# Attention and expert block: order of the prologue, of the second step's sums, and of the x rows and zeros on SyncE's queue

## What is computed

```
q, k, v = x @ wq.T, x @ wk.T, x @ wv.T           # 16 heads of 128
q, k    = rope(rmsnorm(q) * qn), rope(rmsnorm(k) * kn)   # over the head's 128
s       = 50 * tanh(q @ k.T / sqrt(128) / 50);  causal mask
x       = layernorm(x + softmax(s) @ v @ wo.T)
logits  = x @ gate.T     # 32 experts in 8 groups: the 3 best groups, the 6 best experts
x       = layernorm(x + sum of 6 weighted experts (48 places each) + shared expert)
```

## Time and profile before

| | |
|---|---|
| timed runs | 1084.98, 1086.15, 1086.78 us; median 1086.15 |
| profiled execution | 1092.47 us, of which 1090.7 are the span of the trace |
| mean granted TensorE clock | 0.973 |
| TensorE (matmul) busy | 1019.1 us, 93% |
| DVE busy | 850.7 us, 78% |
| ScalarE busy | 698.9 us, 64% |
| GpSimd busy | 647.2 us, 59% |
| HBM read, written | 63.00 MB, 15.75 MB |

### The profile page before, as it was taken

The page is one execution under the profiler, slowest core; times in us unless marked ns, Lnnn a source line. Parts: engine busy times, 40 slices in busy tenths (PEclk is TensorE's granted clock), DMA queues, the critical chain, the costliest instruction groups (busy, mean ns, idle before and its releaser), DMA issues.

```text
span 1090.7 us, 17557 instructions
## 1 busy us (share of the span) xinstructions
PE 1019.1 (93%) x6072; PEld 809.2 (74%) x6072; DVE 850.7 (78%) x1391; ACT 698.9 (64%) x1162; POOL 647.2 (59%) x660
## 2 busy tenths in 40 slices
PE   7799999999999999999999999999999968899966
PEld 5588878887888788888878887888788747345532
DVE  6579898989898889888988898889988865833423
ACT  4667777777777777777777777777777752323212
POOL 2536666666666666666666666666666662365332
PEclk9999999999999999999999999999999987999987
DMA  5610011101110101010101000100000007739937
GB/s 193 238 30 20 31 39 30 62 30 39 31 61 30 41 30 61 31 40 30 62 30 40 31 20 30 40 30 20 21 20 21 21 1 227 209 86 265 237 55 235
DMA packets 52168, 75.42 MB, mean 69 GB/s; under 512 B 8208, under 2 KB 43248, under 8 KB 51952
## 3 DMA queue, kind: packets, MB, share of 16 engines
q1 hardware_dynamic: 48144, 69.30, 20.1%
q0 software_dynamic: 3072, 4.46, 2.2%
q10 hardware_dynamic: 864, 0.54, 0.2%
HBM read 63.00 MB, written 15.75 MB: 72 GB/s over the span
## 4 chain that ended last, share of the span: by engine, by line
PE 67%; DVE 16%; issue 6%; DMA 6%; POOL 2%; ACT 2%; SPq 0%; ACTq 0%; DVEq 0%; POOLq 0%
PE ps L462 19%; PE ps L463 18%; PE ps L464 18%; DVE prob_lo L1230 6%; PE ps L499 5%; DMA acc_rows<-ye,acci 4%; PE ps L676 2%; DVE qraw L1299 2%; POOL pacc L1089 2%; PE ps L720 2%; PE ps L767 1%; DVE qraw L1317 1%; DVE kT_lo L1230 1%; PE ps L716 1%; DVE qhat_lo L1230 1%
## 5 line engine op out<-in xcount | busy, mean ns | idle before, releaser
L1230 DVE TENSOR_TENSOR prob_lo<-praw,prob_hi 128x1024 fp32r<-128x1024 f32 (+7 forms) x256 | 301.4, 1201 | 3.4 <-ACT prob_hi L837 3.4
L1072 POOL TENSOR_SCALAR_AFFINE_SELECT praw<-praw 128x128 f32<-128x128 f32 x256 | 119.5, 467 | 264.4 <-ACT praw L893 261.6
L1089 POOL TENSOR_TENSOR pacc<-pacc,praw 128x768 f32<-128x768 f32 (+2 forms) x192 | 234.6, 1222 | 27.7
L887 ACT ACTIVATE praw<-ps,rk 128x1024 f32<-128x1024 f32 (+7 forms) x256 | 186.2, 741 | 68.8 <-PE ps L464 64.6
L837 ACT ACTIVATE prob_hi<-praw 128x1024 fp32r<-128x1024 f32 (+7 forms) x256 | 168.7, 686 | 1.9 <-POOL praw L1072 1.9
L893 ACT ACTIVATE praw<-praw 128x1024 f32<-128x1024 f32 (+7 forms) x256 | 168.2, 684 | 0.0
L462 PE MATMUL ps<-qhat_hi,kT_hi 128*128 128x512 f32 (+3 forms) x384 | 135.2, 352 | 9.6 <-DVE qhat_lo L1230 9.6
L462 PE MATMUL ps<-prob_hi,vS_hi 128*128 128x512 f32 (+3 forms) x384 | 136.4, 355 | 8.0 <-DVE prob_lo L1230 8.0
L463 PE MATMUL ps<-prob_lo,vS_hi 128*128 128x512 f32 (+3 forms) x384 | 133.9, 349 | 0.0
L464 PE MATMUL ps<-prob_hi,vS_lo 128*128 128x512 f32 (+3 forms) x384 | 133.0, 346 | 0.0
L463 PE MATMUL ps<-qhat_lo,kT_hi 128*128 128x512 f32 (+3 forms) x384 | 132.9, 346 | 0.0
(11 more groups left out here) (167 smaller groups left out, 2240.2 us busy)
## 6 DMA issues: line engine op xcount, KB each, us to landing
qsq<-rq_rows SPq DMA_DIRECT2D x32, 512.0 KB, 4.0
wgu<-in_wgu SPq DMA_DIRECT2D x16, 704.0 KB
wd<-in_wd SPq DMA_DIRECT2D x16, 352.0 KB
acc_rows<-acc_rows SPq DMA_DIRECT2D x8, 544.0 KB, 6.1
acc_rows<-pacc SPq DMA_DIRECT2D x8, 512.0 KB, 9.8
accA<-acc_rows SPq DMA_DIRECT2D x8, 512.0 KB, 5.8
wraw<-in_wqkv SPq DMA_DIRECT2D x15, 256.0 KB, 4.5
wvraw<-in_wqkv SPq DMA_DIRECT2D x16, 128.0 KB, 2.7
```

The lines of the kernel that those rows point to most:

```text
L887: nc.scalar.activation(praw[:, raw_at(b, j)], buf[:, P * j:T], ACT.Tanh, scale=rk[:, b, j:j + 1]).then_inc(tanh_done, 1)
L1072: nc.gpsimd.affine_select(out=diag, in_=diag, compare_op=ALU.is_ge, fill=0.0, base=0, pattern=[[1, P]], channel_multiplier=-1).then_inc(ma ...
L1089: nc.gpsimd.tensor_tensor(pacc[:, P * j:T], before, raw, ALU.add).then_inc(pacc_done, 1)
L1230: v.tensor_tensor(dst, x_, hi.bitcast(F32), ALU.subtract).then_inc(done, 1)
```

## The change

DVE's prologue runs the fold of q's sums right behind q1, and V's weights' split behind that; `turn_rms(0)` follows, then the head scales, then the second head's weights. In the opening, `ss` comes ahead of `vb` in the list, on TensorE ahead of the first scores, and on DVE (with the output weights' split and `turn_rms(1)`) ahead of vb's low part. SyncE loads x's rows behind the broadcast of the second row. Of the zeros the front keeps one write of 256 rows (256 KB) and the one of 144 KB. The other 16 parts of the first table and 17 of the second are copies of those 256 rows, six behind the last broadcast of each of the pairs 1 to 5 and three in pair 6; the first scatter waits for all 33.

```diff
--- before.py
+++ after.py
@@ -42,7 +42,10 @@
 XD = D + E
 ACCR = N + P
 ROUNDS = C // 8
-ZEROS = 16 * ((2 * ACCR // P * D + T - 1) // T + 1)
+ZEROS = 16 * 2
+PARTS = 17
+PART = 2 * ACCR // PARTS
+CLEARS = 2 * PARTS - 1
 NEG = -3.0e38
 POS = 3.0e38
 SR = 2
@@ -74,7 +77,7 @@
 BEHIND = {"sums", "op0", "op1", "op2", "op3"}
 AHEAD = {"q0", "q1", "k0", "k1", "ss"}
 PROLOGUE = "q0 q1 sq k0 k1 vd sk".split()
-OPENING = "k0 k1 va q0 q1 vb ss".split()
+OPENING = "k0 k1 va q0 q1 ss vb".split()
 EARLY = len(PROLOGUE) + len(OPENING)
 EARLY_BANKS = [6, 7, 4, 5]
 SMALL = 4
@@ -288,7 +291,7 @@
         xhi_done, xlo_done = sem("xhi_done"), sem("xlo_done")
         whi_done, wlo_done = sem("whi_done"), sem("wlo_done")
         wq_in, wqhi_done, wqlo_done = sem("wq_in"), sem("wqhi_done"), sem("wqlo_done")
-        sq_folded, side_zeros = sem("sq_folded"), sem("side_zeros")
+        sq_folded, table_zeros = sem("sq_folded"), sem("table_zeros")
         wohi_done, wolo_done = sem("wohi_done"), sem("wolo_done")
         pj_done, pj_free = sem("pj_done"), sem("pj_free")
         wvhi_done, wvlo_done, vhi_done = sem("wvhi_done"), sem("wvlo_done"), sem("vhi_done")
@@ -376,14 +379,15 @@
                 sp.dma_start(rqB[:, :], rq_d[b:b + 1, :].to_broadcast([P, T])).then_inc(rqB_in, 16)
 
             rq_broadcast(0, 0)
-            sp.dma_start(yacc[:, :, :], x_v).then_inc(x_in, 16)
             sp.wait_ge(zeros_set, 1)
             zero = pacc[:, :]
-            rows = acc_d.rearrange("(p r) d -> p (r d)", p=P)
-            for c0 in range(0, 2 * ACCR // P * D, T):
-                cn = min(T, 2 * ACCR // P * D - c0)
-                sp.dma_start(rows[:, c0:c0 + cn], zero[:, 0:cn]).then_inc(zeros_out, 16)
+            sp.dma_start(acc_d[0:PART, :].rearrange("(p r) d -> p (r d)", p=P), zero[:, 0:PART * D // P]).then_inc(zeros_out, 16)
             sp.dma_start(x1_d[N:ACCR, :], zero[:, 0:XD]).then_inc(zeros_out, 16)
+
+            def clear(n):
+
+                table, part = (acc_d, n + 1) if n < PARTS - 1 else (acc2_d, n - PARTS + 1)
+                sp.dma_start(table[PART * part:PART * part + PART, :], acc_d[0:PART, :]).then_inc(table_zeros, 16)
 
             next_wqkv = wqkv_d[2:H].rearrange("(n e) p m c d -> n e p m c d", e=2)
             next_wo = wo_d[2:H].rearrange("(n e) p d -> n e p d", e=2)
@@ -392,6 +396,8 @@
                 for e in range(2):
                     sp.dma_start(wvraw[:, e], next_wqkv[bass.ds(p, 1), e, :, 2].rearrange("o p c d -> p (o c) d")).then_inc(wv_in, 16)
                 rq_broadcast(p * STEPS + 1, 1)
+                if p == 0:
+                    sp.dma_start(yacc[:, :, :], x_v).then_inc(x_in, 16)
                 sp.wait_ge(wlo_done, p * 2 + 2)
                 for e in range(2):
                     sp.dma_start(wraw[:, e], next_wqkv[bass.ds(p, 1), e, :, 0:2].rearrange("o p m c d -> p (o m) c d")).then_inc(w_in[e], 16)
@@ -400,13 +406,12 @@
                 for e in range(2):
                     sp.dma_start(woraw[:, e], next_wo[bass.ds(p, 1), e].rearrange("o p n -> p (o n)")).then_inc(wo_in[e], 16)
                 rq_broadcast(p * STEPS + 3, 1)
-                if 1 <= p < 5:
-                    if p == 1:
-                        sp.wait_ge(zeros_out, ZEROS)
-                    for part in (2 * p - 2, 2 * p - 1):
-                        some = slice(ACCR // 4 * part, ACCR // 4 * part + ACCR // 4)
-                        sp.dma_start(acc2_d[some, :], acc_d[some, :]).then_inc(side_zeros, 16)
                 rq_broadcast(p * STEPS + 4, 0)
+                if p == 0:
+                    sp.wait_ge(zeros_out, ZEROS)
+                else:
+                    for n in range(6 * p - 6, min(6 * p, CLEARS)):
+                        clear(n)
             for q in range(1, STEPS):
                 rq_broadcast((NP_ - 1) * STEPS + q, q % 2)
 
@@ -575,12 +580,12 @@
                 pe.wait_ge(wlo_done, 2)
                 for what in OPENING[:-2]:
                     project(what, 0 if what[0] == "v" else 1, 0, *st.unit(what))
+                sums_of_squares(1, *st.unit("ss"))
                 pe.wait_ge(qlo_done, 1)
                 scores(0, 0, 0)
                 pe.wait_ge(xlo_done, 2 * KC + 1)
                 scores(0, 0, 1)
                 project("vb", 0, 0, *st.unit("vb"))
-                sums_of_squares(1, *st.unit("ss"))
                 for j in (2, 3, 4, 5):
                     scores(0, 0, j)
                 pe.wait_ge(pj_free, st.unit("q1")[0])
@@ -1180,12 +1185,12 @@
 
             def scatter(p):
                 pool.wait_ge(ey_evac, p + 1)
+                if p == 0:
+                    pool.wait_ge(table_zeros, 16 * CLEARS)
                 row = bass.IndirectOffsetOnAxis(ap=acci[:, p:p + 1], axis=0)
                 if p in SIDE:
                     if SIDE.index(p):
                         pool.wait_ge(side_added, 16 * SIDE.index(p))
-                    else:
-                        pool.wait_ge(side_zeros, 16 * 8)
                     nc.gpsimd.indirect_dma_start(acc2_d, row, ye[:, p % 4, :], None, compute_op=ALU.add).then_inc(side_added, 16)
                 else:
                     if MAIN.index(p):
@@ -1354,13 +1359,12 @@
             for h in range(2 * KC):
                 split_x(h)
             split_first_keys()
+            for what in ("q0", "q1", "sq"):
+                at_start(what)
+            split_values_weights(0, None)
+            turn_rms(0)
             head_gains()
-            at_start("q0")
-            split_values_weights(0, None)
-            at_start("q1")
-            at_start("sq")
             split_next_weights(0, 1, None)
-            turn_rms(0)
             for what in ("k0", "k1", "vd", "sk"):
                 at_start(what)
             split_x(2 * KC)
@@ -1409,10 +1413,11 @@
 
             def opening(st):
 
-                for what in ("va", "q0", "q1", "vb", "ss"):
+                for what in ("va", "q0", "q1", "ss"):
                     opens(st, what)
                 split_output_weights(st)
                 turn_rms(1)
+                opens(st, "vb")
                 for j in range(4):
                     tile(0, 0, j)
                 scale_raw(1, 1)
```

## The result

The kernel after took **1078.75 us** (median of 13 timed runs, 1075.91 to 1088.71) where the kernel before took 1087.34 (median of 13 beside them, 1081.23 to 1094.52). The ratio is 0.9932, 95% interval 0.9904 to 0.9959: 7.4 us faster, 4.5 to 10.4. The time lies 3.6 us above the predicted 1075.2, inside the range, and outside the 1074 to 1077 of the forecast itself. The sign was right and the size was too large: 11.0 us were forecast. Two of the later sets held one execution at a far lower granted clock (1254 us of before, 1445 us of e7), and these two are in no median or ratio here.

What follows compares the result with a forecast made beforehand. The prediction took the middle as bound by TensorE at a fixed pace, so front savings carry through; 11.6 - 0.6 = 11.0 us off the 1086.15 median gave 1075.2 us, range 1072.6 to 1079.2.

Steps and rivals of the forecast that it cites:

- the forecast itself: Whole kernel: 1074 to 1077 us around the point 1075.2, given a chance of 0.55.
- What bounds the kernel: Middle: TensorE at a fixed pace, 108.17 us a pair, so savings in the front move the rest one for one.
- Part 1: DVE's prologue: first row writes at 14.1, 2.1 us earlier, and scaled queries 2.2 us earlier.
- Part 2: Second step's sums ahead of first scores: first scores 1.67 us earlier, step 1's scores at 44.3, 10.0 us earlier.
- From there to the steady pace: Step 1's scores to V: V's projection at 47.1, clock gain 1.2, 11.6 us in all, less 0.6 for k1 waiting.
- Rival (e): Output weights' split in step 1 not disturbed: V at 45.7 and no 0.6, 1073.2 us; chance 0.12.
- Rival (a): Clock stays a problem: if it falls around the second scores, 2.4 us come back, 1077.6 us; chance 0.12.
- rival (b): Weights' split: each half waits for a whole GpSimd add of 2.11 us, V at 49.6, 1077.7 us; chance 0.04.
- Part 3: x rows behind the second row: loaded by 43.9 at the latest, when DVE comes; costs 0, up to 1 us.
- Part 4: Zeros moved to copies behind later pairs' last broadcasts: cost taken as 0, ends 0 and 3.3 us.
- the last one of the sum: Final step: 11.0 us off the profiled span also come off the 1086.15 median, as the front hardly differs.

Runs made afterwards that it cites:

- e7: Kernel after with each of the 33 zero copies followed by one more of 256 KB to an unused table; 1078.34 us, ratio 0.9919.
- e11: Kernel after with only DVE's old prologue put back (head scales and V's split ahead of q's sums); 1080.85 us, ratio 0.9936.
- e10: Kernel after with second step's sums back behind its third scores and x rows back behind the first broadcast; 1078.34 us, ratio 0.9917.
- e5: Kernel after with 18 and 12 small unread matmuls filling TensorE's pauses around attention's last sums; 1075.93 us, ratio 0.9910.
- e4: Kernel after with only the second step's sums put back between its third scores and V's unit; 1083.0 us, ratio 0.9975.
- e14: Kernel before, unchanged, fourth profile; no timed median given, last sums of attention at 898.50 us.
- e13: Kernel before, unchanged, third profile; no timed median given, last sums of attention at 894.37 us.
- e9: Kernel before, unchanged, second profile; no timed median given, last sums of attention at 895.74 us.
- e6: Kernel before with 18 and 12 small unread matmuls filling TensorE's pauses around attention's last sums; 1085.0 us, ratio 0.9981.
- e3: Kernel before with only the new orders of DVE and TensorE, x rows and all zeros staying in front; 1084.45 us, ratio 0.9978.
- e1: Kernel after, unchanged, timed and profiled a second time; 1078.55 us, ratio 0.9921.
- e15: Kernel after, unchanged, third profile; no timed median given, last sums of attention at 887.41 us.

## Why the prediction was right where it was, and wrong in its size

**What bounds the kernel.** Right. The middle runs at a fixed pace: 108.1 to 108.2 us a pair in before and after, and what V gains at 47 us is at the last sums to within 1 us.

**Part 1.** Row writes were forecast at 14.1 and went at 14.83, 14.55 and 14.19 in the three executions, each 3.49 us after TensorE began q's sums (11.34, 11.06, 10.70); the differences arose ahead of that. What the part is worth at the end is 0.6 to 1.2 us by e11. The prediction gave no such number, since it booked the first scores' 1.67 us for both parts.

**Part 2.** The steps came as worked out: first scores at 26.26, 25.98 and 25.60 (forecast 25.45), directly behind the 16 small matmuls; second row's writes at 30.14, 29.86, 29.49 (29.6); scaling at 40.78, 40.49, 40.12 (40.5), behind DVE's own work and not behind a DMA; scores of step 1 at 44.68, 44.40, 44.02 (44.3). But the 10.0 us that it credits to this path are a reading of after, not a price of the moved sums: e10 has these sums and the x rows in the old place and the same last sums. What the path needed was the zeros out of its way.

**From there to the steady pace.** V at 47.43, 47.15, 46.77 (47.1), k1's wait 0.32 (0.6), the clock at 1.00. Rival (e) asked for an undisturbed split; in these three it took 2.7 us up to the copy. Rival (a) asked for a low clock; in these three it didn't come. In e5 both came at once, and they cancelled: scores at 45.61, V at 46.97. So V came near the forecast 47.1 there in another way than the one forecast. The forecast had weighed the port rule of the Trainium skill ("SBUF — State Buffer", "SBUF: two separate sides") and held that the trace doesn't bear its strict form out. That was read wrongly. The rule says that whichever starts first keeps the shared ports for its whole instruction and the other is blocked until it ends. A loser that comes late then waits only for what is left, and the 1.36 us fit that: the cast began at 54.18, inside an add of 2.07 us that had begun at 53.3, and ended at 55.54. After's rows fit it to 0.15 us: GpSimd's first add ran from 44.38 for 2.11 us,

```profile
44.38 2.11 POOL L1094 TENSOR_TENSOR pacc<-praw 128x896 f32<-128x896 f32 x1 [0.15 <-POOL pacc L1090]
```

and `wo_lo`, begun 0.03 us later, ended at 46.77, which is the add's end and 0.28 more; alone it takes 0.42. In e10 it began at 45.06, ahead of the add at 45.33, and took 0.42. My sum came out right since only one half of the split met an add, and rival (b) had charged both. The 2.56 us that I carried over were two part waits in before and one nearly whole wait (2.36) in after, so that their agreement is luck.

**Part 3.** Cost 0, as taken. The load took 10.5 us from 32.71 and was in at 43.2; DVE came at 44.0. The 0.8 us between are all there is, and e4 shows the price beyond them: 3.50 us of wait, 5.9 at the last sums.

**Part 4.** Cost 0 (e7).

**The step that failed** is the last one of the sum: "the front hardly differs, so the same 11.0 come off". Against the profiled execution of before the 11.0 is well sized: 898.49 less 888.05, 887.62 and 887.41 is 10.4, 10.9 and 11.1. But the front of before, of which the prediction took a single execution for the kernel, is 894.4 to 898.5 at the last sums in four, with the profiled one at the late end. The two terms of the path that were single draws are the landing of the second row's writes (6.7 us; 3.6 to 6.7 in the five executions with before's front) and the time from the scaling to the queries (7.3 us; 3.3 us in three of the five and 5.1 in e14). So step 1's scores, which the prediction moves from 54.31 by 10.0 us, stand at 47.99 in e13, 49.36 in e9 and 52.59 in e14. By the means the front gained 9.1 us (8.1 with e6), and 7.4 and 8.6 were timed, each to some 3 us either way. A third of the 3.6 us is the base: 1086.15 was a median of three runs, and 13 gave 1087.34. So 1.2 us is the base and 2.4 is the difference between 11.0 and the 8.6 of the medians; about 1.9 of that is the front's mean, and the last half us is within what the timing can tell. A hint stood on the page, though a weak one: the profiled execution took 1092.47 us, 5.7 above the slowest of the timed three, so some stage of it had to be slow. The larger part was in the tail (192.2 us, where e9, e13 and e14 have 187.0 to 187.9), and the front is 1.7 us behind the mean of the four. A wait that is removed takes its spread away too: the gain is what it costs on average, not what it cost once.

## What to carry to other kernels

Before a stall is priced from one profile, ask what its length hangs on. If it is a drain of a queue or the order of two engines within a few tenths of a us, it varies from execution to execution, and one profile can show it at its late end; a second profile of the kernel before would have said so. Parts of a change can hang together and still bring nothing: the late load of x needs the early sums, or it costs 6 us, and the two together bring no more than neither. So measure the pairs as well as the parts, and ask which pair could be dropped whole. And once a late input is gone, look at the next waits in the steady pace: one split moved out of V's way brought as much as the whole change here, since it counts eight times.

## What the runs showed of the hardware

Four writes of 1 KB each landed 2.2 us after their issue on a queue without bulk ahead of them, and 3.6 to 9.6 us after it behind 4.4 MB of zeros. Issued 6.9 us earlier (29.55 in e3, 36.47 in e13) they landed 1.7 us earlier (39.14, 40.85): they wait for the drain.

An instruction of DVE on SBUF beside an add of GpSimd was held for the rest of that add: 0.42 us became 2.36, and 0.3 us of order decided. DVE's copies from PSUM beside the same adds kept their 0.64 us (1.28 for two at 46.70).

The granted clock in the tail differed between executions of one kernel: 0.53 to 0.62 over 910 to 930 us in one, 1.00 in the other, TensorE being busy for most of both. In the front it fell in e5 behind a pause of 1.50 us (0.66 over 35 to 40 us) and stayed at 1.00 behind the same pause in after, e1, e15 and e7. It was at 1.00 behind the pause of 3.06 us in before.
